# A two-layer kernel: transposed input loaded instead of turned, modulation in row tiles, and the tile carries moved from VectorE to ScalarE and GpSimd

## The reference

```
# layer 0, y = x + block0(x)
ctx    = ema(x, tau_ctx)                          # h = alpha*h + x over time
gated  = x * sigmoid([x, ctx] @ Wg.T + bg)
h1     = gelu(x @ Wn1.T + bn1)                    # 32 values per step
mod    = 0.5 + sigmoid(h1 @ Wn2.T + bn2)          # 32 modulations per step
traces = ema(gated * mod[d], tau[d])              # d = 0..31, one decay each
temporal = sum_d traces[d] * softmax(blend)[d]
soma   = gelu(x @ Wsoma.T);  gate = sigmoid(temporal @ Wtemp.T)
block0 = layernorm((soma * gate) @ Wout.T)
# layer 1, out = y + block1(y)
Q, K, V = y @ Wq.T, y @ Wk.T, y @ Wv.T            # 16 heads
block1 = softmax(Q K.T * scale + bias) V @ Wo.T   # sparse by index counts, or dense
```

## Time and profile before

| | before |
|---|---|
| three runs | 368.14, 373.5, 380.67 us |
| profiled execution, its own time | 366.06 us |
| its span | 364.3 us |
| mean granted TensorE clock | 0.959 |
| busy TensorE, VectorE, ScalarE, GpSimd | 86%, 82%, 59%, 65% |
| layer 0, `front` to the last step | 0 to 181.5 us |
| end of layer 0 beside the first octets | 181.5 to about 213 us |
| octets of layer 1 alone | about 213 to 364.3 us |

### The profile page before, as it was taken

The page is one execution under the profiler, slowest core; times in us unless marked ns, Lnnn a source line. Parts: engine busy times, 40 slices in busy tenths (PEclk is TensorE's granted clock), DMA queues, the critical chain, the costliest instruction groups (busy, mean ns, idle before and its releaser), DMA issues. The chain is left out here.

```text
span 364.3 us, 10344 instructions
## 1 busy us (share of the span) xinstructions
PE 311.9 (86%) x3351; PEld 213.7 (59%) x3361; DVE 296.9 (82%) x1530; ACT 213.2 (59%) x452; POOL 236.9 (65%) x281
## 2 busy tenths in 40 slices
PE   1769559998999989898938499899899989999994
PEld 0425227565564746564524466777687768777772
DVE  4775997979797878879784877799799989999971
ACT  5833201565646364554705367787688868888772
POOL 2045143464655566564733497699899999999980
PEclk9969788999999999999978989999999999999998
DMA  7101000101001035100552004425544564454011
GB/s 206 48 0 31 0 0 2 30 4 29 2 0 31 3 87 94 20 0 0 74 70 32 0 4 86 91 62 71 141 102 98 82 131 104 98 78 103 3 31 30
DMA packets 23473, 18.91 MB, mean 52 GB/s; under 512 B 2304, under 2 KB 23040, under 8 KB 23424
## 3 DMA queue, kind: packets, MB, share of 16 engines
q1 hardware_dynamic: 23424, 18.31, 25.0%
HBM read 3.62 MB, written 2.10 MB: 16 GB/s over the span
## 5 line engine op out<-in xcount | busy, mean ns | idle before, releaser
L1411 POOL TENSOR_TENSOR arena<-arena,neg_max 128x512 f32<-128x512 f32 x128 | 130.1, 1050 | 21.5 <-DVE neg_max L1285 21.2
L1285 DVE CUSTOM_DVE_ANT_0 arena<-ps,arena 128x128 f32<-128x128 f32 x512 | 113.8, 286 | 13.4 <-PE ps L655 7.5
L934 ACT ACTIVATE arena<-ps 128x512 f32<-128x512 f32 x128 | 69.7, 596 | 16.3 <-PE ps L669 16.3
L669 PE MATMUL ps<-ident_sb,arena 128*128 128x128 f32 x512 | 69.1, 279 | 0.0
L1371 POOL TENSOR_TENSOR arena<-arena 128x448 f32<-128x448 f32 (+6 forms) x56 | 41.8, 746 | 29.9 <-DVE arena L1113 27.4
L669 PEld LDWEIGHTS ps<-ident_sb,arena 128*128 128x128 f32 x512 | 57.0, 142 | 6.6 <-issue 4.2
L1358 POOL TENSOR_TENSOR arena<-decay_a,arena 128x192 f32<-128x192 f32 x32 | 22.3, 717 | 38.5 <-ACT arena L794 38.5
L1285 DVE DVE_READ_ACCUMULATOR2_ANT neg_max<- 128x1 f32 x512 | 42.5, 83 | 0.0
L685 PE MATMUL ps<-arena 128*32 128x128 f32 x1024 | 41.5, 280 | 0.0
L1113 DVE TENSOR_TENSOR arena<-ps,arena 128x448 f32<-128x448 f32 (+6 forms) x56 | 23.5, 426 | 14.2 <-PE ps L456 8.7
L655 PE MATMUL ps<-arena 48*128 48x128 bf16 x512 | 25.7, 220 | 8.3 <-DVE neg_max L1285 5.7
(11 more groups left out here) (154 smaller groups left out, 594.5 us busy)
## 6 DMA issues: line engine op xcount, KB each, us to landing
arena<-q_parts SPq DMA_DIRECT2D x96, 64.0 KB
arena<-k_parts SPq DMA_DIRECT2D x96, 64.0 KB
arena<-in_x SPq DMA_DIRECT2D x8, 256.0 KB, 2.8
out<-arena SPq DMA_DIRECT2D x8, 256.0 KB, 3.0
w_sb<-in_w SPq DMA_DIRECT2D x1, 576.0 KB, 6.5
arena<-in_consts SPq DMA_DIRECT2D x1, 420.0 KB, 5.5
rows_sb<-in_rows SPq DMA_DIRECT2D x1, 288.5 KB, 3.0
ident_sb<-in_ident SPq DMA_DIRECT2D x1, 64.0 KB, 3.1
```

The source lines that it names most:

```text
L669: mm = pe.transpose(ps[1][:, q % 2, k * P:k * P + P], neg_t[q % NT_RING][:, k * P:k * P + P], ident)
L934: act.activation(probT[q % PT_RING], ps[1][:, q % 2, :], ACT.Exp, scale=-1.0)\
L1285: dve.tensor_tensor_reduce(out=neg_t[q % NT_RING][:, cs], in0=ps[0][:, score_bank(c) + slot, cs], in1=nbias[n % 2], scale=1.0, scalar=3.0e ...
L1411: pool.tensor_tensor(t4, t4, neg_max[:, n % 2, 4 * z:4 * z + 4].unsqueeze(2).broadcast_to([P, 4, P]), ALU.subtract).then_inc(s["shifted"], 1)
```

## The change

- The host passes x transposed as well (`xt`). SyncE loads both forms of each group, and `f_x` goes on TensorE (four transposes) and ScalarE (a copy). The load of the transposed tile waits for `cross_ps` of two groups before, since the tile lies under `bh`.
- Modulation uses the 32 rows of weights that matter, as two pairs of matmuls (`half` 0 and 1) on different row groups in different banks, with the gate's matmuls between them. `wn2_row` and its copies go.
- VectorE no longer multiplies the carries. ScalarE copies them from PSUM into `carry_sb`, and GpSimd does the three products at the head of its step.
- The order of a step is new on TensorE, ScalarE and VectorE; the first two `bias_terms`, `row_values` and `bias_sum` move from `end` into step 2.

```diff
 # SyncE
+                sp.wait_ge(s["cross_ps"], grp(i, m, 1, -1))
+                sp.dma_start(by_row(xT[m % 2]), xt[:, group_rows(i, m), :]).then_inc(s[f"xT_loaded{m % 2}"], 16)
...
 # TensorE
+                for k in range(2):
+                    b = 2 * half + k
+                    rows_of = slice(b * D, b * D + D)
+                    mm = pe.matmul(mod_banks(u)[:, k, half * P:half * P + P], wn2_sb[rows_of, :],
+                                   h1T[u][rows_of, :], start=True, stop=True)
...
             def step(i, m):
-                f_x(i, m + 1)
                 f_context(i, m + 1)
+                f_soma(i, m + 1)
+                f_hidden(i, m + 1)
                 b_carries(i, m)
-                f_soma(i, m + 1)
-                f_gate(i, m + 1)
-                f_hidden(i, m + 1)
+                f_modulation(i, m + 1, 0)
+                f_gate_x(i, m + 1)
+                f_modulation(i, m + 1, 1)
+                f_gate_ctx(i, m + 1)
                 b_locals(i, m)
...
 # ScalarE
+            def b_carries(i, m):
+                u = m % 2
+                act.wait_ge(s["carry_ps"], grp(i, m, 1, 1))
...
+                act.activation(carry_sb[0:NCAR * D, :], bank(u, 3)[0:NCAR * D, :], ACT.Copy)\
+                    .then_inc(s["carry_copied"], 1)
...
 # VectorE
             def step(i, m):
                 closes, counts = not at_start(i, m, 1), at_start(i, m, 1)
-                b_carries(i, m)
                 if closes:
                     c_residual(i, m - 1)
                 if counts:
                     neighbours()
-                    one_hots(0, 8)
+                    one_hots(0, 4)
+                f_modulation(i, m + 1)
                 f_gated(i, m + 1)
                 b_locals(i, m)
+                f_mod_parts(i, m + 1)
                 if counts:
-                    one_hots(8, 12)
-                f_modulation(i, m + 1)
+                    one_hots(4, 12)
                 b_temporal(i, m)
...
 # GpSimd
+            def b_carries(i, m):
...
+                pool.wait_ge(s["carry_copied"], grp(i, m, 1, 1))
+                for j in range(1, NJ):
+                    rows_of = slice((j - 1) * D, j * D)
+                    pool.tensor_tensor(by_row(bh[u][NLOC * D:P, j, :]), by_row(carry_sb[rows_of, :]),
+                                       blend_of(rows_of), ALU.mult).then_inc(s["carried"], 1)
+
+                    pool.wait_ge(s["carried"], grp(i, m, NCAR, j))
...
             def step(i, m):
+                b_carries(i, m)
                 f_inputs(i, m + 1)
```

More of the change, by code:

```diff
@@ L63 @@
 C_END = C_K + P
-VEC_STEPS = ["neg_abs_tau", "neg_relu_tau", "gate_biases", "mod_bias", "q_bias", "k_bias"] + [f"wn2_row{b}" for b in range(GB)] + ["log_decay", "lt",
+VEC_STEPS = ["neg_abs_tau", "neg_relu_tau", "gate_biases", "mod_bias", "q_bias", "k_bias"] + ["log_decay", "lt",
              "blend_max", "blend_negmax", "decay_arg", "blend_sum", "blend_recip", "blend_4", "half_bw", "decay_p",
@@ L80, in scal, with build @@
     return ACT_STEPS.index(name) + 1
-def build(nc, x, w, wn2, cols, rows, consts, ident_in, idx, masks, out):
+def build(nc, x, xt, w, wn2, cols, rows, consts, ident_in, idx, masks, out):
     with ExitStack() as ctx:
@@ L254, in by_row, with blend_of @@
             return ap.rearrange("p (b c) -> p b c", b=GB)
+        def blend_of(rows_of):
+            return half_bw[rows_of, :].unsqueeze(1).broadcast_to([rows_of.stop - rows_of.start, GB, P])
         def each_row(ap):
@@ L531, in c_x1T, with c_k @@
                 turned(closing_bank(i, m, 3), x1g[u], "x1T_ps")
+            def c_k(i, m):
+                pe.wait_ge(s["x1T_ready"], grp(i, m, 1, 1))
+                pe.matmul(closing_bank(i, m, 3), wt["wk"], x1T, start=True, stop=True).then_inc(s["k_ps"], 1)
             def c_q(i, m):
@@ L802, in f_gated @@
                 act.activation(gn[u], bank(u, 2), ACT.Copy).then_inc(s["gn_ready"], 1)
+            def b_carries(i, m):
+                u = m % 2
+                act.wait_ge(s["carry_ps"], grp(i, m, 1, 1))
+                if not at_start(i, m, 1):
+                    act.wait_ge(s["carried"], grp(i, m, NCAR, 0))
+                act.activation(carry_sb[0:NCAR * D, :], bank(u, 3)[0:NCAR * D, :], ACT.Copy)\
+                    .then_inc(s["carry_copied"], 1)
             def b_cross(i, m):
@@ L887, in step @@
                     act.activation(lncnt[:], cnt1[:], ACT.Ln).then_inc(s["lncnt_ready"], 1)
+                if at_start(i, m, 3) and m == 2:
+                    for n in range(2):
+                        bias_terms(n)
+                        row_values(n)
             def bias_terms(n):
@@ L915, in end @@
             def end():
-                for n in range(2):
-                    bias_terms(n)
-                    row_values(n)
+                b_carries(LAST, 1)
                 b_cross(LAST, 1)
@@ L1401, in step @@
                 c_rstd(i, m)
+                if at_start(i, m, 3) and m == 2:
+                    bias_sum(0)
+                    bias_sum(1)
+                    pool.wait_ge(s["bias_ready"], 2)
             def bias_sum(n):
```

182 lines of the change are left out of this document (91 added, 91 removed).

## The result

| | before | after |
|---|---|---|
| runs | 368.14, 373.5, 380.57, 380.67 us | 389.56, 391.97, 392.49, 393.46 us |
| median | 377.03 us | 392.23 us |
| ratio after / before, interval | | 1.0645, 1.0545 to 1.0745 |
| profiled execution, its own time | 366.06 us | 389.56 us |
| its span | 364.3 us | 387.8 us |

The change makes the kernel slower. The ratio leaves out runs more than 1.5% above the fastest of their kernel, which leaves 368.14 us alone of the kernel before, so it lies above the 1.040 of the two medians and hangs on one run. Forecast were +11.7 us (3.1%); the profiled executions differ by 23.5 us.

A forecast was written before the change was run, and what follows sets the result against it. VectorE sets the pace up to the first lag product, then TensorE and VectorE together. -0.5 + 0 + 1.5 + 12.5 - 1.8 = +11.7 us on 366.06 gives 378, plus 7.4 to the median: 385 us, range 363 to 395.

The forecast's parts named there:

- the turns: Loop step: VectorE's SBUF-only and GpSimd's instructions alternate, each waiting for the other's whole one; locals end at 13.7, not 10.6.
- the term of the loop: Layer 0's loop: steps of 22.8 us instead of 20.26, +2.5 on five steps, 12.5 us.
- (1): No interference: GpSimd's new work fits in its idle time; sum -8.3, 365 us; chance 0.18.
- (2): Only two-input VectorE instructions wait, L1119 and L1120 pass; step 21.5 us, sum about +5, 378 us; chance 0.20.
- The race: Loop step: GpSimd's second product comes 0.1 us ahead of VectorE's L1119; the other way round the step is 22.3 us.
- the main line: Loop step with GpSimd's second product ahead of L1119: locals end at 13.7, lag products start at 16.9, step 23.0 us.
- rival (3): Loop: TensorE's granted clock falls to 0.83 in the longer steps; +20, 393 us; chance 0.10.
- The step without interference: Loop step in the new order if VectorE and GpSimd don't hinder each other: 20.0 us, a gain of 0.3.
- Steps 0 and 1: Layer 0's first two steps: the turns take back step 0's gain, 0; later locals in step 1, +1.5 us.
- The end: End of layer 0: carries leave VectorE, cross starts when GpSimd's products end at 188.9 instead of 190.82; -1.8 us.
- The prologue: Before step 0: four copies leave VectorE, log_decay can use about 0.5; -0.5 us, earlier transposes covered by the weights' load.
- Layer 1 unchanged: Octets of layer 1, from about 213 us to the end: nothing in them changes, 0 us.

The follow-up runs named there:

- dvecarry: The changed kernel with the carries' products back on VectorE at the head of its step, reading PSUM; ratio to the kernel before 1.033, median 382.58 us.
- narrow_all: The changed kernel with GpSimd's products, xb and keep on 32 of 512 columns, nothing moved; 376.86 us.
- fill_again: The changed kernel with two spare float32 matmuls in TensorE's wait for gated, timed; 383.64 us profiled, median 389.47 us.
- before_third: The kernel before, unchanged, executed once more for its trace; 368.91 us.
- fill: The changed kernel with two spare float32 matmuls in TensorE's wait for gated, earlier execution; total time not given, step 0 started at 31.93 us.

## Why the prediction was right in direction and short in size

The forecast was 385 us, slower by 3.1%; measured were 392.23, slower by 4.0% of the medians and 6.4% by the ratio. The mechanism named, the turns, is there, and it is half of what a step at full clock lost (1.5 of 2.8 us). The step of the prediction that failed is the term of the loop, "+2.5 on five steps, 12.5 us": the four steps that can be read alone cost 3.6 us each, 14.4 in all, in both pairs of profiles. Step by step:

- *The turns.* Right. L1119, L1120 and L1113 wait at 1.05, 1.48 and 1.76 us (longer than the means near 1.3 for L1120 and 1.1 for L1113 that were named as signs), the locals end at t = 13.67 (13.7), the step at full clock is 23.07 to 23.18 (23.0). That the TENSOR_SCALAR with one SBUF input waits too was an inference; these rows settle it. The Trainium skill (SBUF — State Buffer, Who interferes with whom) says that `tensor_scalar` can, and the traces here agree: 1482 ns beside the products, 420 without them. Strict they are not (`dvecarry`), which the forecast didn't need here, since GpSimd was first each time. Rivals (1) and (2) are out.
- *The race* between the second product and L1119 goes the way of the main line, in all steps read. The 22.8 that was taken as a mean over both outcomes was 0.3 too low, 1.5 us over five steps.
- *The clock* was rival (3), with the right effect in the wrong measure: it falls not throughout, for +20, but in two of five steps, behind the wait for gated, for 1.5 us each. The term above left the clock at nothing: the prediction named TensorE's waiting for gated as a sign (3 us, measured 1.9) and didn't ask what the clock does behind that wait. Of the 4.4 us between 14.4 and 10.0, 1.2 are the 0.3 above and 3.0 the clock, shown by filling that wait.
- *The step without interference*, 20.0, was 1.6 too short (21.6 in `narrow_all`): 0.8 by the halves, the gate's products and the carries on TensorE, 0.8 by q ahead of the cross. It would have spoilt rival (1)'s 365 us: with the new order alone the kernel would have been slower still, as `dvecarry` with a ratio of 1.033 is. So the 3.0 us that the prediction gave to the turns are 1.5 of turns and 1.6 of the new order. That 23.0 came out right was luck: the two overlap, and GpSimd's turns end later than the gate's tanh and q.
- *Steps 0 and 1*: 0 and +1.5 forecast, +0.3 and +1.3 measured.
- *The end*: -1.8 for a cross that starts when GpSimd's products are done. It does wait for them (4.75 us, against the rows of the end), but they start at 206.37, 1.3 us after ScalarE's copy was done at 205.04, and take 4.55 us for the 3.9 forecast. Together with step 6 it is +1.8 for a forecast of +0.7.
- *The prologue*, -0.5: +2.5 in this pair, and not the change's own, since equal programs start at 28.3 or 31.9. "Both earlier transposes are covered" was neither shown nor refuted.
- *Layer 1 unchanged*: right; the reference execution was 3.3 and 3.5 us faster there than two later ones. Adding +11.7 to one execution's time takes all its luck along. `fill_again` against `before_third`, both with an early start and a layer 1 of 144 to 145 us, are 383.64 - 368.91 = 14.7 us apart.

Open: the three other runs of the changed kernel took 2.4 to 3.9 us more than the profiled one at a mean clock of 0.933 to 0.936 instead of 0.957. No trace shows where.

## What to carry to other kernels

Before work goes from VectorE to an idle GpSimd, lay both timelines side by side: in these traces each of GpSimd's additions and products, once begun, made the VectorE instruction on SBUF alone that came beside it wait for its end (those that read PSUM did not), and moving it made it meet the next one. Then ask what TensorE does in the wait that this makes, since its clock may fall to 1.2 GHz just behind it. And compare stretches, not totals, with at least two profiled executions of either kernel, before a few microseconds are put down to a change.

## What was not expected of the hardware

- GpSimd's product on 32 x 512 took 1.26 us, on 128 x 512 1.27; on 32 x 32 it took 0.246 and on 128 x 32 0.25. Its time goes with the columns and not with the partitions.
- A wait of 1.9 us of TensorE in a step that is otherwise busy was followed by 1.2 GHz for k and q, in every second step in four executions (8 of 16); with the wait filled, in none of eight. The clock was still at 1.00 during the wait.
- GpSimd's xb, coming 0.2 to 0.3 us after a VectorE instruction had begun, waited for three of them in a row (`dvecarry`, 2.29 us on average); GpSimd once begun let none pass.
- Two executions of one program (`fill`, `fill_again`) started step 0 at 31.93 and 28.35 us; in the pair of rows above the difference lies in when TensorE first gets 2.4 GHz.
- Two pairs of 128-column matmuls on different row groups took 0.42 us up to the next matmul's start, twice what half of the old modulation's columns suggested, and the gate product between them 1.05 us, where two of its kind in a row are 0.86 apart.
